# Twelve sublayers of a decoder on one core: in seven stage functions ScalarE, and no longer VectorE, scales the normalised rows

## The chip, the cores and the metric

The kernel runs on one core of a Trainium2 chip, in one launch. The metric is the device time of that launch in microseconds (us), lower is better; it is given as the median of several runs. A core has TensorE (matmuls and transposes, "PE" in the profile; "PEld" is its weight load), VectorE ("DVE"), ScalarE ("ACT"), GpSimd ("POOL") and SyncE ("SP", which here only issues transfers). Each engine takes its own instructions in the order in which they were put into its queue, and waits for another engine only through semaphores.

## What is computed

The reference takes `x` (4 rows of a batch, 512 positions, 128 channels, float32) through four layers of three sublayers. Every sublayer has the form below, with a normalisation over the 128 channels that has neither gain nor offset:

```python
def _layernorm(x, axis=-1, eps=1e-05):
    m = jnp.mean(x, axis=axis, keepdims=True)
    v = jnp.var(x, axis=axis, keepdims=True)
    return (x - m) / jnp.sqrt(v + eps)
...
x = x + sublayer(_layernorm(x))
```

The twelve sublayers, in order, with the name that their function has in the kernel: attention of a few selected queries (`l0_attn`), cross-attention with 77 context positions (`cross_attn`), local attention and a small feed-forward net, each twice (`f0_attn`, `f0_mlp`); attention (`l1_attn`), cross-attention (`cross_attn`), eight experts with a second normalisation inside (`l1_ffn`); attention over compressed, selected and windowed keys (`l2_attn`), masked cross-attention (`cross_attn`), a mixture of experts (`l2_ffn`); a selective scan (`l3_attn`), differential cross-attention (`l3_xattn`) and a last feed-forward net (`l3_ffn`). The sublayers mix positions of one row of the batch, never two rows. The data is in float32.

## The kernel before

**Two lanes.** The four rows of the batch are worked on by two lanes: lane 0 takes rows 0 and 2, lane 1 rows 1 and 3. Each lane has buffers and four banks of PSUM of its own. A lane goes through a layer's stages for one of its rows, then for the other one. `x` of all rows stays in SBUF, positions on the partitions: four tiles of 128 positions by 128 channels in each row of the batch. Most stages first need the normalised row transposed, channels on the partitions, which is `xnT` (128x512).

**The normalisation** has this chain, in `norm_stats`, `norm_pool`, `norm_apply`, `norm_tensor` and `norm_scalar`:

1. VectorE: `BN_STATS` of the four tiles (L467), then `BN_AGGR` of the four (L471), which gives mean and variance in `mv`.
2. GpSimd: variance plus epsilon in `vare` (L478), then to the power -1/2 in `rstd` (L479), both on 128x4 numbers.
3. VectorE: four times `tensor_scalar`, (x - mean) * rstd, 128x128 each, into `xn` (L487).
4. TensorE: four transposes into a bank of PSUM (L495), each as soon as its tile of `xn` is there.
5. ScalarE: one copy 128x512 from PSUM to `xnT` (L502).

**Who sets the order.** A stage function returns one generator for each engine. Each `yield` ends a piece; a piece begins with its waits. Before any instruction is issued, the generators of both lanes are run once against stand-ins of the engines (class `Meter`, and `Pool` for GpSimd), which only note waits, estimated costs (VectorE 0.18 us + 0.00104 us for each element of the width in a `tensor_scalar`, ScalarE 0.18 us + 0.00084 us in an activation, GpSimd 0.25 us + 0.002 us) and signals. `plan()` then runs a small greedy simulation: at each step it takes, among the next pieces of both lanes on all engines, the one that can begin first by these estimates. The order that results is the order in which the pieces are put into the queues of the engines. On the chip it is fixed: a piece whose wait isn't over holds up everything behind it on its engine, of the other lane too.

```python
                found.append((max(p[0], free[k[0]]), p[0] + p[1], k, p))
        begin, _, k, (_, took, signals, to) = min(found, key=lambda c: c[:2])
```

**Other lines that are spoken of.** L639 to L651 are VectorE's part of `l0_attn`: the value rows, then a search for the largest query norms (copy L642, MAX, MAX_INDEX and MATCH_REPLACE from L645, index map L651). L691 is its closing addition to `x`, L807 the row maximum of the first cross-attention. L724, L757 to L764 are the products and ScalarE's copies of cross-attention. L1149 is an activation of the small feed-forward net of layer 0. L1345 is GpSimd's memset of a value buffer in `l1_attn`. L1607, L1968, L2295 and L2483 are the closing additions of `l1_ffn`, `l2_attn`, `l3_attn` and `l3_xattn`. In `l3_attn` GpSimd multiplies (L2210), VectorE scans (L2277), and L2194 is the exponential on ScalarE.

## Time and profile before

| | |
|---|---|
| time, median of 3 runs | 2674.53 us (2669.82 to 2679.3) |
| the profiled execution: its time | 2670.86 us |
| the profiled execution: its span | 2669.0 us |
| TensorE busy | 1970.7 us, 74% |
| VectorE busy | 1740.5 us, 65% |
| ScalarE busy | 1016.6 us, 38% |
| GpSimd busy | 693.3 us, 26% |
| mean granted clock of TensorE | 0.815 of full speed |

The profile shows one execution. Its span goes from the first to the last recorded instruction; its time is 1.9 us longer. Busy shares are means over twelve stages with different limits. They don't say which engine ends a wait in a given stage, so the trace has to be read by stretches of time. A mean granted clock of 0.815 is a mean over stretches at full speed and at half of it.

### The profile page before, as it was taken

The page shows a single profiled execution, that of the slowest core. Times are in us where ns is not written, and L with a number is a line of the kernel's source. Part 1 is how long each engine was busy: PE and PEld are TensorE (multiplying, and loading weights), DVE is VectorE, ACT ScalarE, POOL GpSimd, SP SyncE. Part 2 cuts the span into 40 slices and gives each one's busy share as a digit, 9 for nine tenths or more (in the row PEclk, how much of TensorE's full clock was granted, in tenths as well). Part 3 has the DMA queues.
Part 4 walks back from the last instruction along what each step waited for, and adds up shares of the span by engine and source line. Part 5 has one row for each costly group of instructions (what it writes and reads, how often), then busy time and mean ns, then how long its engine had stood idle before and what let it go on. Part 6 is the DMA issues. An engine that isn't in the chain of part 4 may idle for free. (4 is left out here: it accounts for less than half of the span.)

```text
span 2669.0 us, 31475 instructions
## 1 busy us (share of the span) xinstructions
PE 1970.7 (74%) x11471; PEld 1135.5 (43%) x11474; DVE 1740.5 (65%) x3786; ACT 1016.6 (38%) x1606; POOL 693.3 (26%) x548
## 2 busy tenths in 40 slices
PE   4787888878777777799997577668866656677753
PEld 2453645445452232367665455545412222234331
DVE  6645657564655454433637787964579889986876
ACT  0235454555544343333333232232353544333422
POOL 0002323231320010000002443520136436445520
PEclk8787888989996686789998778766677877888875
DMA  3002111120220000000000000000000000000000
GB/s 148 1 1 52 40 48 44 32 60 23 69 83 1 1 1 1 12 10 1 1 1 1 1 1 1 1 1 1 0 0 0 0 0 0 1 1 1 1 5 12
DMA packets 19225, 43.86 MB, mean 16 GB/s; under 512 B 5323, under 2 KB 7935, under 8 KB 18175
## 3 DMA queue, kind: packets, MB, share of 16 engines
q1 hardware_dynamic: 19071, 41.86, 5.6%
q8 instruction: 91, 1.49, 0.2%
q14 instruction: 63, 0.52, 0.1%
HBM read 16.67 MB, written 1.05 MB: 7 GB/s over the span
## 5 line engine op out<-in xcount | busy, mean ns | idle before, releaser
L478 POOL TENSOR_SCALAR lane_vare<-lane_mv 128x4 f32<-128x4 f32 x64 | 18.0, 282 | 1098.0 <-DVE lane_mv L471 1097.9
L2134 PE MATMUL lane_banks<-l_attn_lane_hc,base 128*128 128x512 f32 x256 | 169.9, 781 | 114.2 <-DVE l_attn_lane_hc L2286 114.1
L2210 POOL TENSOR_TENSOR l_attn_lane_u<-l_attn_lane_xp,l_attn_lane_bn 128x512 f32<-128x512 f32 x128 | 181.2, 1441 | 228.6 <-ACT l_attn_lane_bn L2186 224.2
L2277 DVE TENSOR_TENSOR_SCAN l_attn_lane_h<-l_attn_lane_da,l_attn_lane_u 128x512 f32<-128x512 f32 x128 | 191.4, 1524 | 4.1 <-POOL l_attn_lane_u L2210 2.8
L1334 ACT ACTIVATE l_attn_lane_ex<-lane_banks 128x768 f32<-128x768 f32 (+3 forms) x128 | 86.8, 702 | 159.6 <-PE lane_banks L1292 158.9
L1526 ACT ACTIVATE l_ffn_lane_hT<-lane_banks,weights 128x512 f32<-128x512 f32 x128 | 87.9, 687 | 151.1 <-PE lane_banks L1482 150.6
L2134 PEld LDWEIGHTS lane_banks<-l_attn_lane_hc,base 128*128 128x128 f32 x256 | 56.8, 241 | 191.7 <-DVE l_attn_lane_hc L2286 156.8
L1573 DVE SCALAR_TENSOR_TENSOR l_ffn_lane_eo<-lane_banks,l_ffn_lane_sel,l_ffn_lane_eo 128x128 f32<-128x128 f32 x224 | 63.0, 344 | 110.0 <-PE lane_banks L1504 110.0
L1504 PEld LDWEIGHTS lane_banks<-weights,l_ffn_lane_hT 128*128 128x128 f32 x1024 | 120.5, 192 | 26.8 <-issue 24.8
L1504 PE MATMUL lane_banks<-weights,l_ffn_lane_hT 128*128 128x128 f32 x1024 | 123.4, 277 | 8.3 <-DVE l_ffn_lane_eo L1573 6.6
L2342 PE MATMUL lane_banks<-l_xattn_lane_km,l_xattn_lane_qT 128*128 128x462 f32 (+1 forms) x192 | 96.1, 604 | 41.2 <-DVE l_xattn_lane_sc L2455 33.8
L2186 ACT ACTIVATE l_attn_lane_bn<-lane_banks 128x512 f32<-128x512 f32 x64 | 38.1, 596 | 209.0 <-PE lane_banks L2128 205.8
L1831 POOL TENSOR_TENSOR l_attn_lane_qb<-l_attn_lane_qT,base 128x512 f32<-128x512 f32 x64 | 84.5, 1333 | 103.9 <-PE lane_banks L1733 66.5
L873 PE MATMUL lane_banks<-f_attn_lane_work,weights 128*128 128x512 f32 x128 | 76.9, 721 | 32.7 <-ACT f_attn_lane_work L988 32.7
L1394 DVE TENSOR_REDUCE l_attn_lane_mx<-lane_banks 128x4 f32<-128x2048 f32 (+2 forms) x64 | 93.2, 1487 | 9.2 <-PE lane_banks L1273 8.9
L1027 POOL TENSOR_TENSOR f_attn_lane_work<-f_attn_lane_work,f_attn_lane_rden 128x512 f32<-128x512 f32 x64 | 66.4, 1041 | 108.7 <-DVE f_attn_lane_rden L1071 108.7
L1742 PE MATMUL lane_banks<-base,l_attn_lane_sc 128*112 128x128 f32 x256 | 53.1, 345 | 53.2 <-POOL l_attn_lane_sc L1844 48.9
L1379 DVE RECIPROCAL l_attn_lane_rden<-lane_banks 128x16 f32<-128x16 f32 x16 | 4.1, 253 | 133.1 <-PE lane_banks L1244 133.1
L2194 ACT ACTIVATE l_attn_lane_da<-l_attn_lane_dt,a 128x512 f32<-128x512 f32 x128 | 86.4, 714 | 4.8 <-DVE l_attn_lane_h L2277 4.7
L1733 PE MATMUL lane_banks<-l_attn_lane_kall,l_attn_lane_qb 128*128 128x112 f32 x512 | 78.9, 307 | 11.2 <-DVE l_attn_lane_sc L1957 8.6
L487 DVE TENSOR_SCALAR lane_xn<-x,lane_mv,lane_rstd 128x128 f32<-128x128 f32 x176 | 61.6, 443 | 37.0 <-POOL lane_rstd L479 36.9
L2286 DVE TENSOR_TENSOR l_attn_lane_hc<-l_attn_lane_h,lane_banks 128x512 f32<-128x512 f32 x128 | 81.4, 671 | 4.3 <-PE lane_banks L2136 4.1
(518 smaller groups left out, 4972.1 us busy)
## 6 DMA issues: line engine op xcount, KB each, us to landing
f_attn_lane_work<-f_attn_lane_work SPq DMA_DIRECT2D x256, 64.0 KB, 2.0
weights<-packed SPq DMA_DIRECT2D x1, 4564.5 KB, 19.9
f_attn_lane_vb<-f_attn_lane_va SPq DMA_DIRECT2D x8, 512.0 KB, 4.5
f_attn_lane_vb<-f_attn_lane_va SPq DMA_DIRECT2D x8, 384.0 KB, 5.8
weights<-packed SPq DMA_DIRECT2D x1, 2320.0 KB, 8.0
weights<-packed SPq DMA_DIRECT2D x1, 2091.0 KB, 13.2
out<-x SPq DMA_DIRECT2D x4, 256.0 KB, 2.4
weights<-packed SPq DMA_DIRECT2D x1, 897.0 KB, 9.5
```

Of the source, the lines that this page charges most:

```text
L1334: act.activation(ex[:, kt % 2, h:h + 2, 0:T - P * kt], banks(0, 2)[:, :, 0:T - P * kt], ACT.Exp, scale=scale)\
L1394: v.tensor_reduce(mx[:, j, t, :], banks(0, R)[:, :, 0:n], AX.X, ALU.max).then_inc(*s.up("row_max"))
L1504: last = pe.matmul(ps(2)[:, tile(t)], hT[:, n % 2, c, tile(t)], w("m1_w2", (2 * (e - 1) + c) * D, (2 * (e - 1) + c + 1) * D), start=(c == ...
L1526: act.activation(hT[:, n % 2, c, :], ps(c), ACT.Relu, bias=w("m1_b1", b, b + 1)).then_inc(*s.up("hidden_ready"))
L1733: last = pe.matmul(ps(j % 2)[:, g * C:(g + 1) * C], qb[:, j % 2, tile(g)], kall[:, j, :], start=True, stop=True)
L1831: g_.tensor_tensor(qb[:, j % 2, :].rearrange("p (h q) -> p h q", h=A2_H), bc(qT[:, 32 * j:32 * j + 32], A2_H), w("headmask").rearrange("p ...
L2134: pe.matmul(ps(2 + c), w("ident"), hc[:, c, :], start=(n == 1), stop=(n == NS)).then_inc(*s.up("state_added"))
L2194: act.activation(da[:, i % 3, :], dt[:, c, :], ACT.Exp, scale=net.a3[:, c, n:n + 1]).then_inc(*s.up("da_ready"))
L2210: g.tensor_tensor(u[:, i % 3, :], dtx[:, c, :], bn[:, n % 2, :], ALU.mult).then_inc(*s.up("u_ready"))
L2277: v.tensor_tensor_scan(h[:, c, :], da[:, i % 3, :], u[:, i % 3, :], 0.0, ALU.mult, ALU.add).then_inc(*s.up("scanned"))
L2286: v.tensor_tensor(hc[:, c, :], h[:, c, :], ps(1), ALU.mult).then_inc(*s.up("hc_ready"))
L2342: pe.matmul(score_bank(u), qT[:, tile(t)], km[:, half * H + lo:half * H + hi, :].rearrange("p m k -> p (m k)"), start=True, stop=True).the ...
```

## The change

In seven stage functions (`l0_attn`, `cross_attn`, `l1_attn`, `l1_ffn`, `l2_attn`, `l2_ffn`, `l3_xattn`; `cross_attn` serves three stages) step 3 of the chain leaves VectorE. GpSimd works out `less` = -mean (128x4) before L478, and after L479 multiplies it by `rstd` in a piece of its own, which waits for `rstd_ready`. ScalarE then computes the four tiles of `xn` as Identity(rstd * x + less), with scale and bias taken from columns of one number a partition. That is 9 stages times 4 rows, 36 normalisations and 144 tiles. `l3_attn`, `f0_attn`, `f0_mlp`, `l3_ffn` and the inner normalisation of `l1_ffn` keep the form before. All numbers of lines below L500 grow by 7 to 16.

```diff
-def norm_pool(ln, s, g, tag=""):
+def norm_pool(ln, s, g, tag="", center=False):
+
     yield
     g.wait_ge(*s.at(tag + "variance_ready", 1))
+    if center:
+        ln.pool_steps.step(g.tensor_scalar(ln.less[:, :], ln.mv[:, :, 0], -1.0, None, ALU.mult))
     ln.pool_steps.link(g.tensor_scalar(ln.vare[:, :], ln.mv[:, :, 1], LN_EPS, 0.0, ALU.add, ALU.add))
     g.tensor_tensor(ln.rstd[:, :], ln.vare[:, :], ln.net.w("neghalf", 0, NT), ALU.pow).then_inc(*s.up(tag + "rstd_ready"))
+    if center:
+        yield
+        g.wait_ge(*s.at(tag + "rstd_ready", 1))
+        g.tensor_tensor(ln.less[:, :], ln.less[:, :], ln.rstd[:, :], ALU.mult).then_inc(*s.up(tag + "less_ready"))
...
+def norm_scale(ln, s, act, src):
+    yield
+    act.wait_ge(*s.at("less_ready", 1))
+    for t in range(NT):
+        act.activation(ln.xn[:, t, :], src[:, t, :], ACT.Identity, scale=ln.rstd[:, t:t + 1], bias=ln.less[:, t:t + 1])\
+           .then_inc(*s.up("norm_ready"))
...
     def scalar(act):
         enter(act)
+        yield from norm_scale(ln, s, act, x)
         yield from norm_scalar(ln, s, act, ps(0))
...
     def gpsimd(g):
         enter(g)
-        yield from norm_pool(ln, s, g)
+        yield from norm_pool(ln, s, g, center=True)
         g.memset(va[:, :, :, A1_HD + 1:32], 0.0).then_inc(*s.up("va_zeroed"))
         g.memset(va[:, :, :, A1_HD:A1_HD + 1], 1.0).then_inc(*s.up("va_zeroed"))
...
         yield from norm_stats(ln, s, v, x)
-        yield from norm_apply(ln, s, v, x, ln.xn)
```

The last three hunks are those of `l1_attn`; the other six functions differ in the same three places. In `l1_attn` the memsets now stand behind GpSimd's second wait. In the cross-attentions `norm_scale` stands behind the copies of the keys.

The planner is given the new pieces with their estimates, so its simulation comes out otherwise from the first stage on, and all engines' orders change with it. Three places follow, all on VectorE. Names are those of the buffers (`lane_` and `l_attn_lane_` are of either lane).

The first is the first pair of rows in `l0_attn`, at the program's start. Before:

```order
L467 BN_STATS lane_bn<-x 128x6 x4
L471 BN_AGGR lane_mv<-lane_bn 128x2 x4
L639 TENSOR_TENSOR l_attn_lane_v<-lane_banks,weights 128x512
L487 TENSOR_SCALAR lane_xn<-x,lane_mv,lane_rstd 128x128 x4
L642 COPY l_attn_lane_qn<-lane_banks 16x512
L645 MAX l_attn_lane_top<-l_attn_lane_qn 16x8
```

Changed (L661 to L667 are L645 to L651 before, L472 is L471, L673 builds the selection matrix):

```order
L661 MAX l_attn_lane_top<-l_attn_lane_qn 16x8
L662 MAX_INDEX l_attn_lane_topi<-l_attn_lane_top,l_attn_lane_qn 16x8
L665 CAST l_attn_lane_topf<-l_attn_lane_topi 16x32
L666 MEMSET l_attn_lane_topf 16x1
L667 TENSOR_TENSOR l_attn_lane_idxd<-weights,l_attn_lane_topf 16x512
L472 BN_AGGR lane_mv<-lane_bn 128x2 x4
L673 TENSOR_SCALAR l_attn_lane_onehot<-lane_banks,base 128x512 x4
```

The second lane's `BN_AGGR`, which stood ahead of the first lane's search, now stands behind all of it.

The second is the first rows' end of `l2_attn`. Before, the first lane's closing addition L1968 and, 49 rows further on, the second lane's:

```order
L1965 TENSOR_TENSOR x<-x,weights 128x512
L1968 TENSOR_TENSOR x<-x,lane_banks 128x512
L467 BN_STATS lane_bn<-x 128x6 x4
L471 BN_AGGR lane_mv<-lane_bn 128x2 x4
L1957 TENSOR_TENSOR l_attn_lane_sc<-lane_banks,l_attn_lane_mask 128x448
L487 TENSOR_SCALAR lane_xn<-x,lane_mv,lane_rstd 128x128 x4
```

```order
L1943 TENSOR_TENSOR l_attn_lane_tokens<-lane_banks,weights 128x512
L1947 TENSOR_REDUCE l_attn_lane_oT<-l_attn_lane_tokens 128x128
L1965 TENSOR_TENSOR x<-x,weights 128x512
L1957 TENSOR_TENSOR l_attn_lane_sc<-lane_banks,l_attn_lane_mask 128x448 x2
L1968 TENSOR_TENSOR x<-x,lane_banks 128x512
```

Changed (L1984 is L1968 before, L1959 and L1963 are L1943 and L1947, L468 is L467); directly ahead of these rows stands the first lane's L1984:

```order
L468 BN_STATS lane_bn<-x 128x6 x4
L472 BN_AGGR lane_mv<-lane_bn 128x2 x4
L1959 TENSOR_TENSOR l_attn_lane_tokens<-lane_banks,weights 128x512
L1963 TENSOR_REDUCE l_attn_lane_oT<-l_attn_lane_tokens 128x128
L1959 TENSOR_TENSOR l_attn_lane_tokens<-lane_banks,weights 128x512
L1963 TENSOR_REDUCE l_attn_lane_oT<-l_attn_lane_tokens 128x128
L1981 TENSOR_TENSOR x<-x,weights 128x512
L1870 TENSOR_TENSOR l_attn_lane_turns<-lane_banks,weights 128x512
L1871 TENSOR_TENSOR l_attn_lane_turns<-lane_banks,weights 128x512
L1872 TENSOR_TENSOR l_attn_lane_kp<-l_attn_lane_turns 128x512
L1881 COPY l_attn_lane_gl_172<-lane_banks 32x48
L1984 TENSOR_TENSOR x<-x,lane_banks 128x512
```

The second lane's closing addition now stands 12 rows behind the first lane's, where it stood 53 rows behind. Counted in the same way over the program, the closing additions of `l3_attn` (L2295) stand at rows 1701, 1770, 1851 and 1917 before and 1649, 1676, 1769 and 1799 after; those of `l3_xattn` (L2483) at 2008, 2046, 2142 and 2201 before and 1913, 1924, 2028 and 2042 after.

## Rows read from the trace of the kernel before

**Rows 1.** Busy time in four stretches (from:to, length, engines, clock, DMA share, GB/s):

```profile
1156.00:1282.00 126.00, 123.36 (x685) 87.64 (x684) 51.47 (x206) 47.11 (x72) 2.54 (x4) 0.96 0.02 6
1438.00:1576.00 138.00, 85.81 (x667) 66.91 (x665) 112.28 (x229) 35.62 (x50) 60.67 (x38) 0.75 0.00 1
2587.00:2628.00 41.00, 17.05 (x83) 7.71 (x84) 37.83 (x132) 10.57 (x18) 2.53 (x4) 0.56 0.02 7
2628.00:2669.00 41.00, 9.89 (x51) 4.55 (x52) 21.15 (x72) 6.12 (x10) 1.27 (x2) 0.50 0.07 20
```

**Rows 2.** The page's groups, VectorE's scaling (busy us, mean ns | idle before):

```profile
L487 DVE TENSOR_SCALAR lane_xn<-x,lane_mv,lane_rstd 128x128 f32<-128x128 f32 x176 | 61.6, 443 | 37.0 <-POOL lane_rstd L479 36.9
```

**Rows 3.** Timelines, one chain in the first cross-attention (start, length, instruction, [wait before]):

```profile
169.67 0.24 POOL L478 TENSOR_SCALAR lane_vare<-lane_mv 128x4 f32<-128x4 f32 x1 [69.60 <-DVE lane_mv L471]
169.99 1.03 POOL L479 TENSOR_TENSOR lane_rstd<-lane_vare,base 128x4 f32<-128x4 f32 x1
171.12 1.12 DVE L487 TENSOR_SCALAR lane_xn<-x,lane_mv,lane_rstd 128x128 f32<-128x128 f32 x4 [0.25 <-POOL lane_rstd L479]
172.66 0.60 ACT L502 ACTIVATE lane_xnT<-lane_banks 128x512 f32<-128x512 f32 x1 [0.93 <-PE lane_banks L495]
```

**Rows 4.** Groups by line and shape, ScalarE, activations with one or two operands more:

```profile
L1149 ACT ACTIVATE f_mlp_lane_hT<-lane_banks,weights 128x512 f32<-128x512 f32 x8 | 6.2, 777 | 25.0 <-PE lane_banks L495 25.0
L760 ACT ACTIVATE cross_attn_lane_kT<-lane_banks 128x77 f32<-128x77 f32 x8 | 1.9, 235 | 11.9 <-PE lane_banks L718 11.9
L757 ACT ACTIVATE cross_attn_lane_kT<-lane_banks,weights 128x77 f32<-128x77 f32 x4 | 1.3, 326 | 21.2 <-PE lane_banks L718 21.2
L758 ACT ACTIVATE cross_attn_lane_kT<-cross_attn_lane_kT,weights 128x77 f32<-128x77 f32 x4 | 1.4, 360 | 0.1
```

**Rows 5.** Timelines, `l1_attn` and `l2_ffn`, long scalings and what GpSimd did:

```profile
945.37 1.33 POOL L1345 MEMSET l_attn_lane_va<- 128x1472 f32 x1
945.56 2.07 DVE L487 TENSOR_SCALAR lane_xn<-x,lane_mv,lane_rstd 128x128 f32<-128x128 f32 x4
1767.22 3.96 DVE L487 TENSOR_SCALAR lane_xn<-x,lane_mv,lane_rstd 128x128 f32<-128x128 f32 x4 [1.37 <-POOL lane_rstd L479]
```

**Rows 6.** Waits, VectorE from 1438 to 2587 us (idle us, waits, longest):

```profile
DVE lane_xn L487 <- POOL lane_rstd L479: 16.4, 14, 1.9
```

**Rows 7.** Timeline, VectorE, the first rows in `l0_attn` and the first cross-attention:

```profile
24.67 0.38 DVE L471 BATCH_NORM_AGGREGATE lane_mv<-lane_bn 128x2 f32<-128x6 f32 x4
40.02 0.68 DVE L651 TENSOR_TENSOR l_attn_lane_idxd<-weights,l_attn_lane_topf 16x512 f32<-16x512 f32 x1
170.19 0.69 DVE L691 TENSOR_TENSOR x<-x,lane_banks 128x512 f32<-128x512 f32 x1 [0.71 <-PE lane_banks L599]
176.28 0.48 DVE L807 TENSOR_REDUCE cross_attn_lane_mx<-lane_banks 128x4 f32<-128x308 f32 x1 [3.07 <-PE lane_banks L729]
```

**Rows 8.** Timeline, VectorE, closing additions of both lanes:

```profile
2070.81 0.68 DVE L2295 TENSOR_TENSOR x<-x,lane_banks 128x512 f32<-128x512 f32 x1
2144.82 0.69 DVE L2295 TENSOR_TENSOR x<-x,lane_banks 128x512 f32<-128x512 f32 x1 [0.87 <-PE lane_banks L2142]
2549.64 0.69 DVE L2483 TENSOR_TENSOR x<-x,lane_banks 128x512 f32<-128x512 f32 x1 [8.77 <-PE lane_banks L2379]
2586.38 0.69 DVE L2483 TENSOR_TENSOR x<-x,lane_banks 128x512 f32<-128x512 f32 x1 [4.97 <-PE lane_banks L2379]
```

**Rows 9.** Busy time of VectorE's scans L2277 alone, two stretches (busy us, count, clock):

```profile
2001.00:2063.00 62.00, 44.32 (x28) 0.78 0.00 0
2063.00:2128.00 65.00, 19.80 (x16) 0.82 0.00 1
```

**Rows 10.** Timeline, ScalarE in `l3_attn`, around one table load:

```profile
1970.78 0.71 ACT L2194 ACTIVATE l_attn_lane_da<-l_attn_lane_dt,a 128x512 f32<-128x512 f32 x1
1971.51 1.28 ACT L2164 ACT_TABLE_LOAD   x1
1972.80 0.63 ACT L2164 ACTIVATE l_attn_lane_sgc<-l_attn_lane_cv 128x512 f32<-128x512 f32 x1
```

More of the change, by code:

```diff
@@ L315, in __init__ @@
         self.rstd = net.sb(f"lane{index}_rstd", [P, NT])
+        self.less = net.sb(f"lane{index}_less", [P, NT])
         self.area = net.take(SCRATCH)
@@ L635, in vector @@
         yield from norm_stats(ln, s, v_, x)
-        yield from norm_apply(ln, s, v_, x, ln.xn)
         yield
@@ L760, in scalar @@
             act.activation(kT[:, :], ps(1, 0, S2), ACT.Copy).then_inc(*s.up("k_ready"))
+        yield from norm_scale(ln, s, act, x)
         yield from norm_scalar(ln, s, act, ps(0))
@@ L780, in gpsimd @@
         enter(g)
-        yield from norm_pool(ln, s, g)
+        yield from norm_pool(ln, s, g, center=True)
     def vector(v):
@@ L1306, in scalar @@
         enter(act)
+        yield from norm_scale(ln, s, act, x)
         yield from norm_scalar(ln, s, act, ps(0))
@@ L1343, in gpsimd @@
         enter(g)
-        yield from norm_pool(ln, s, g)
+        yield from norm_pool(ln, s, g, center=True)
         g.memset(va[:, :, :, A1_HD + 1:32], 0.0).then_inc(*s.up("va_zeroed"))
@@ L1358, in vector @@
         yield from norm_stats(ln, s, v, x)
-        yield from norm_apply(ln, s, v, x, ln.xn)
         for i, name in enumerate("qk"):
@@ L1510, in scalar @@
         enter(act)
+        yield from norm_scale(ln, s, act, x)
         yield from norm_scalar(ln, s, act, ps(0))
@@ L1537, in gpsimd @@
         enter(g)
-        yield from norm_pool(ln, s, g)
+        yield from norm_pool(ln, s, g, center=True)
         yield from norm_pool(ln, s, g, tag="out_")
@@ L1544, in vector @@
         yield from norm_stats(ln, s, v, x)
-        yield from norm_apply(ln, s, v, x, ln.xn)
         def logits():
@@ L1772, in scalar @@
         act.activation(mask[:, :, 0:C - A2_M], w("a2_seen").rearrange("p (j k) -> p j k", j=J), ACT.Copy).then_inc(*s.up("seen_ready"))
+        yield from norm_scale(ln, s, act, x)
         yield from norm_scalar(ln, s, act, ps(0))
@@ L1822, in gpsimd @@
         enter(g_)
-        yield from norm_pool(ln, s, g_)
+        yield from norm_pool(ln, s, g_, center=True)
         g_.memset(kp[:, 0:32], 0.0).then_inc(*s.up("pad_ready"))
@@ L1850, in vector @@
         yield from norm_stats(ln, s, v, x)
-        yield from norm_apply(ln, s, v, x, ln.xn)
         def rope(dst, signal):
@@ L2025, in scalar @@
         enter(act)
+        yield from norm_scale(ln, s, act, x)
         yield from norm_scalar(ln, s, act, ps(0))
@@ L2039, in gpsimd @@
         enter(g)
-        yield from norm_pool(ln, s, g)
+        yield from norm_pool(ln, s, g, center=True)
     def vector(v):
@@ L2045, in vector @@
         yield from norm_stats(ln, s, v, x)
-        yield from norm_apply(ln, s, v, x, ln.xn)
         yield
@@ L2386, in scalar @@
         act.activation(kT[:, :], ps(1, 0, S2), ACT.Identity, bias=w("x3_bk")).then_inc(*s.up("k_ready"))
+        yield from norm_scale(ln, s, act, x)
         yield from norm_scalar(ln, s, act, ps(0))
@@ L2413, in gpsimd @@
         g.memset(va[:, :, :], 0.0).then_inc(*s.up("va_zeroed"))
-        yield from norm_pool(ln, s, g)
+        yield from norm_pool(ln, s, g, center=True)
         for i in range(UNITS + 2):
@@ L2430, in vector @@
         yield from norm_stats(ln, s, v, x)
-        yield from norm_apply(ln, s, v, x, ln.xn)
         yield
```

## The prediction

> **What bounds the kernel now.** I read the busy shares first (the table above). No engine is near its span: TensorE 74%, VectorE 65%, ScalarE 38%, GpSimd 26%. So the limit changes with the stage, and I cut the span into stretches [rows 1]. The reader is to see three kinds. In the experts of layer 1 TensorE works 123.36 of 126 us; nothing taken from VectorE can help there. In `l2_attn` VectorE works 112.28 of 138 us (81%) and TensorE 85.81; there VectorE's queue is the nearest to a limit. In the last 82 us everything waits for everything: at first VectorE is busy 37.83 of 41 us with both lanes, then, with one lane alone, only 21.15 of 41.
>
> Next the chain of the normalisation itself. The page's groups give all scalings into `xn`: 176 tiles, 61.6 us of VectorE, and 37.0 us of idle time ahead of them, 36.9 of it for GpSimd's power [rows 2]. 36 of its 44 groups of four change, 144 tiles, so 50 us (61.6 x 144/176) leave VectorE, 1.9% of the span. One chain in time order [rows 3]: L478 takes 0.24 us, L479 1.03, four scalings 1.12, and `xnT` is done at 173.26, 3.6 us after L478 began. A wait for `rstd` ends on every engine that has nothing else queued; where the lanes go in step, this chain lies on the path.
>
> **The change, part by part.** Every duration is of the profiled execution, and the sum is made against its time of 2670.9 us. That is 3.7 us under the median of 2674.5, so a result is moved up by 3.7 at the end.
>
> *One chain's latency.* GpSimd's `less` = -mean has the form of L478, so +0.24 us [rows 3]. The product with `rstd` isn't in the trace in this form on 128x4; it lies between L478's 0.24 and L479's 1.03, and as it has no power I take 0.24 plus 0.08, the gap between L478's end and L479's start: +0.32. ScalarE's Identity with both operands on 128x128 isn't in the trace either. A copy costs 0.60 us at 512 wide [rows 3] and 235 ns at 77 wide, so about 277 ns at 128. Scale and bias add 777 - 600 = 177 ns at 512 wide, the bias alone 326 - 235 = 91 ns, and with SBUF as source it is 360 where a bias costs 326, 34 more [rows 4]. 277 + 177 + 34 = 0.49 us a tile. Four lie between 1.7 us (overlapping like VectorE's) and 2.0 us (end to end), against 1.12: +0.6 to +0.9. I take +0.6, since the transposes follow tile by tile. A chain thus grows by 1.2 us, bounds 0.8 and 2.2 (the product at 1.03, the tiles end to end).
>
> (a) *Stages in which the lanes go in step* (`l0_attn`, first and second cross-attention, `l1_attn`, `l1_ffn`): ten pairs of chains, of which a pair exposes one. In the two pairs of `l1_ffn` TensorE at 98% hides it [rows 1]. Eight times 1.2 is +9 us. Against it: in `l1_attn` a scaling took 2.07 us beside GpSimd's memset of 1.33 us [rows 5], 0.95 more than the usual 1.12. The memset now comes after the product and ScalarE does the scaling. Four such, two exposed: -2. Together +7.
>
> (b) *Stages in which they don't* (`l2_attn`, third cross-attention, `l2_ffn`, `l3_xattn`): 16 chains. VectorE gets back 16 x 1.12 = 18 us. In this part of the span it waited 16.4 us for the power before the scalings [rows 6]; 16 of the 20 chains there change, so 13 us go. Of the 61.6 us, 44 x 1.12 = 49.3 are the usual time; 12.3 are longer ones, 3.8 of that in `l1_attn`, and of the rest I give these stages a good half, 5 us (the longest took 3.96 [rows 5]). In all 36 us. VectorE is busy 81% there, so the most that can reach the end is 29, and nothing is possible too, as the lane whose chain it is doesn't get its rows sooner. I take half, 18. The chains' own growth, 16 x 1.2 = 19 us, lies under the other lane's work but for VectorE's idle fifth: +4. Together -14.
>
> (c) *The early order.* The second lane's `BN_AGGR` ran at 24.67 and will now run behind the first lane's search, which ended at 40.70 [rows 7]: up to 16 us later. Most of it was waiting for the same search anyway. What is newly uncovered is the lane's way from variance to its own search: 3.6 us up to `xnT` [rows 3] and some 2.4 for product, copy and sum, so +6. In the cross-attentions the second lane's closing addition, at 170.19, will stand behind the first lane's row maximum, which ended at 176.76 [rows 7]: 5.9 us later at most, but the addition's lane has GpSimd, transposes and products of its own to go through beside the other's; I take +1 for each of two pairs. Together +8, bounds 2 and 25. GpSimd, ScalarE and TensorE have the second lane's chain queued behind this wait, nothing of the first lane's before its selection.
>
> (d) *The late order.* From `l2_attn` on the lanes stand closer: 12 rows instead of 53. At the end they were 36.7 us and 59 rows apart [rows 8], now 14 rows. Alone, the last lane leaves VectorE idle 48% of the time [rows 1]. The part spent alone shrinks by 36.7 x 45/59 = 28 us, and at that idle share 28 x 0.48 = 13 us are saved; with its share for lost `l3_xattn` waits I take -16 (bounds 0 and -28). The price is in `l3_attn`, where the lanes were 74 us apart [rows 8], one lane's products beside the other's scans. With both scanning a scan takes 44.32/28 = 1.58 us, with one 19.80/16 = 1.24 [rows 9]. If the new order puts 40 to 65 more of the scans beside the other lane's, that is +14 to +22; I take a bit over half of the lower, +8, because the order says who stands beside whom but not for how long. Together -8.
>
> The changed kernel's order has eight table loads fewer on ScalarE, all in `l3_attn`. A load takes 1.28 us, and the activation before it ended at 1971.49, the one after began at 1972.80: 1.31 us from the one to the other [rows 10]. That is 10 us of an engine which is busy under half of the time there, and I count nothing. The Trainium skill (ScalarE: Activation LUTs, What ACT_TABLE_LOAD costs) puts a drain of 1380 ns on top, 2.66 us a switch; eight would be 21 us and, if a fifth of it showed, 4 us less in the sum. These rows leave no room for such a drain.
>
> Sum: +7 - 14 + 8 - 8 = -7: 2664 for a profiled run, **2667 us** as a median.
>
> **The rivals.**
>
> *A. The relief counts in full.* For it: VectorE at 81% in `l2_attn`, and 37 us of idle time that no longer exist. Against it: the other engines wait in the same chain. Then (b) is -29 + 4, (d) is -16, table loads half their 10: +7 - 25 + 8 - 16 - 5 = -31, 2640, as a median 2643; between 2630 and 2652.
>
> *B. Slower: scans in step.* One mechanism, in `l3_attn`: both lanes arrive together, scan together and do their products together. 65 scans more at 0.34 us are +22, and the stretch in which one prepares while the other scans, which kept VectorE at work (19.80 us of scans in 65), falls away: +10 for the two rounds. The tail's gain halves, -8. With (a) +7, (b) -14 and (c) +8: +25, 2696, as a median 2699; between 2688 and 2705. It decides from about 45 more scans in step on. For it: the closing additions of `l3_attn` are 27 and 30 rows apart instead of 69 and 66. Against it: the planner's own costs see VectorE's queue. The Trainium skill speaks for this rival (GPSIMD Engine Reference, 1. Specifications): GpSimd shares its SBUF interfaces with VectorE and contends with its instructions that have two SBUF inputs, as a scan has. The scans' 1.58 beside 1.24 us agree.
>
> *C. ScalarE's queue.* The scaling now waits for GpSimd at the head of ScalarE's queue, and the other lane's exponentials and copies stand behind it; before, ScalarE waited only for the transposes. 36 times 1.2 us, half of it felt, is +22 in place of part (b)'s +4: +11 on the whole, 2682, as a median 2685; between 2678 and 2692. Against it: ScalarE has 35.62 us in 138 of `l2_attn` [rows 1].
>
> *D. Nothing to see.* A reordering of 2669 us of work for 50 us of one engine ends within 8 us of before: 2667 to 2682.
>
> **How the numbers follow.** Forecast (2655 to 2680) 0.38, A 0.20, B 0.22, C 0.10, D 0.10. 0.3% is 8 us, about what a measurement of this kernel tells from no change: 2666.5 and 2682.5. Faster: A's 0.20, half of the forecast (0.19), a little of D: 0.41. Slower: B 0.22, C 0.08, the bounds of (c): 0.32. The same: 0.27. The range leaves out A's lower third and B's upper quarter, with some 0.05 for what I haven't seen: 2640 to 2698.
>
> **What would show it.** Right: four scalings on ScalarE in 1.7 to 2.0 us, a product of about 0.3 us; the second lane's first `BN_AGGR` after 40 us; the end of `l0_attn` some 6 us later; from `l2_attn` to the end a stretch shorter by about 20 us; a tail alone of about 15 us. Wrong: scans at a mean near 1.58 through all of `l3_attn` (B); VectorE waiting longer for ScalarE's copies in `l2_attn` than before (C); the kernel level with before up to `l3_attn` (a and c too dear); the lanes drifting apart on the chip although the order has them close (d).

## The result, and the profile after

The changed kernel takes 2714.5 us (median of 4 runs, 2714.0 to 2719.9) where the kernel before takes 2674.7. The ratio is 1.0154, 95% interval 1.0132 to 1.0176: slower by 1.5%, some 40 us. The forecast was 2667 with a range up to 2698.

The page's busy times, and then the page's groups of the changed normalisation:

```profile
PE 2007.0 (74%) x11471; PEld 1158.7 (43%) x11474; DVE 1690.0 (62%) x3642; ACT 1061.4 (39%) x1742; POOL 718.9 (26%) x620
```

```profile
L503 ACT ACTIVATE lane_xn<-x,lane_less,lane_rstd 128x128 f32<-128x128 f32 x144 | 59.2, 482 | 107.5 <-POOL lane_less L487 107.5
L487 POOL TENSOR_TENSOR lane_less<-lane_less,lane_rstd 128x4 f32<-128x4 f32 x36 | 9.9, 274 | 3.0 <-POOL lane_rstd L483 0.2
```

VectorE fell by 50.5 us, from 1740.5 to 1690.0, as forecast. A tile costs ScalarE 482 ns, where the forecast had 490. What the forecast had no term for is the first number: TensorE is busy 36.3 us longer, with the same 11471 matmuls. Some of that is the choice of run: the changed kernel's profiled run, at 2719.9 us and a granted clock of 0.798, is the longest of its four, and that of the kernel before, at 0.815, is below its median.

The chain in the first cross-attention, timelines of GpSimd, ScalarE, VectorE and TensorE (to be read beside [rows 3, 7]):

```profile
177.76 0.69 DVE L707 TENSOR_TENSOR x<-x,lane_banks 128x512 f32<-128x512 f32 x1 [3.46 <-PE lane_banks L615]
179.68 0.26 DVE L810 COPY cross_attn_lane_vt<-lane_banks 77x128 f32<-77x128 f32 x1
179.95 0.24 POOL L481 TENSOR_SCALAR lane_less<-lane_mv 128x4 f32<-128x4 f32 x1 [71.02 <-DVE lane_mv L472]
180.27 0.24 POOL L482 TENSOR_SCALAR lane_vare<-lane_mv 128x4 f32<-128x4 f32 x1
180.59 1.04 POOL L483 TENSOR_TENSOR lane_rstd<-lane_vare,base 128x4 f32<-128x4 f32 x1
181.71 0.20 POOL L487 TENSOR_TENSOR lane_less<-lane_less,lane_rstd 128x4 f32<-128x4 f32 x1
181.94 1.65 ACT L503 ACTIVATE lane_xn<-x,lane_less,lane_rstd 128x128 f32<-128x128 f32 x4 [2.59 <-POOL lane_less L487]
184.80 2.07 PE L740 MATMUL lane_banks<-lane_xnT,weights 128*128 128x512 f32 x2 [0.69 <-ACT lane_xnT L518]
189.59 0.48 DVE L823 TENSOR_REDUCE cross_attn_lane_mx<-lane_banks 128x4 f32<-128x308 f32 x1 [9.65 <-PE lane_banks L745]
190.18 0.68 DVE L707 TENSOR_TENSOR x<-x,lane_banks 128x512 f32<-128x512 f32 x1
```

GpSimd's part now takes 1.96 us (179.95 to 181.91) instead of 1.35, the four tiles 1.65 instead of 1.12. VectorE copies the values right after the statistics, then stands idle 9.65 us for the scores, and only then closes the second lane's `l0_attn`: 12.4 us after the first lane's, where 2.7 us lay between them before. VectorE's waits for the scores, in all cross-attentions that wait in this way (idle us, waits, longest), before and changed:

```profile
DVE cross_attn_lane_mx L807 <- PE lane_banks L729: 41.7, 8, 6.7
```

```profile
DVE cross_attn_lane_mx L823 <- PE lane_banks L745: 76.2, 8, 9.9
```

That growth has two sources. In the experiments below the changed work in before's order (oldorder_newwork) waits 60.9 us, and before's work in nearly all of the changed order (neworder_oldwork) waits 47.0. In this order:

```profile
DVE cross_attn_lane_mx L852 <- PE lane_banks L773: 60.9, 8, 9.2
```

```profile
DVE cross_attn_lane_mx L852 <- PE lane_banks L773: 47.0, 8, 6.9
```

**Where the time went, by stage.** I took the mean of both lanes' closing additions as a stage's end, for two profiled runs 49 us apart (2669.0 and 2718.1). `l0_attn` of the first rows: +9.5. From there to the end of the first feed-forward: +3.7, and +3.0 for its second rows. `l1_attn` +4.2, second cross-attention +10.7, `l1_ffn` +11.0, `l2_attn` -1.4, third cross-attention and `l2_ffn` -8.4, `l3_attn` +19, `l3_xattn` -4.8, the rest +2.6. There is no single place. At the end of the second cross-attention both lanes are 31 us late. From `l1_ffn` on the changed order brings the lanes closer together, and then the split depends on the measure: by the later lane alone `l3_attn` is +12 and the rest +14. Only the sum of these stages, +18, can be used there.

### The profile page after: what moved, and what is told of

Same layout as the page of the kernel before. It is cut to its first block and busy times, and to the rows that moved or that the text cites. A ratio compares the mean times of both kernels' runs of the same rounds, so it can differ in the third digit from the quotient of the medians.

```text
span 2718.1 us, 31517 instructions
## 1 busy us (share of the span) xinstructions
PE 2007.0 (74%) x11471; PEld 1158.7 (43%) x11474; DVE 1690.0 (62%) x3642; ACT 1061.4 (39%) x1742; POOL 718.9 (26%) x620
## 5 line engine op out<-in xcount | busy, mean ns | idle before, releaser
L2226 POOL TENSOR_TENSOR l_attn_lane_u<-l_attn_lane_xp,l_attn_lane_bn 128x512 f32<-128x512 f32 x128 | 189.3, 1509 | 150.5 <-ACT l_attn_lane_bn L2202 140.7
L481 POOL TENSOR_SCALAR lane_less<-lane_mv 128x4 f32<-128x4 f32 x36 | 11.4, 316 | 705.2 <-DVE lane_mv L472 704.9
L2293 DVE TENSOR_TENSOR_SCAN l_attn_lane_h<-l_attn_lane_da,l_attn_lane_u 128x512 f32<-128x512 f32 x128 | 194.0, 1559 | 4.0 <-ACT l_attn_lane_da L2210 1.9
L2358 PE MATMUL lane_banks<-l_xattn_lane_km,l_xattn_lane_qT 128*128 128x462 f32 (+1 forms) x192 | 93.4, 595 | 14.3 <-DVE l_xattn_lane_sc L2471 12.7
L503 ACT ACTIVATE lane_xn<-x,lane_less,lane_rstd 128x128 f32<-128x128 f32 x144 | 59.2, 482 | 107.5 <-POOL lane_less L487 107.5
L1758 PE MATMUL lane_banks<-base,l_attn_lane_sc 128*112 128x128 f32 x256 | 56.6, 364 | 55.7 <-POOL l_attn_lane_sc L1861 50.5
```

Source lines behind the costliest of these rows:

```text
L2226: g.tensor_tensor(u[:, i % 3, :], dtx[:, c, :], bn[:, n % 2, :], ALU.mult).then_inc(*s.up("u_ready"))
L2293: v.tensor_tensor_scan(h[:, c, :], da[:, i % 3, :], u[:, i % 3, :], 0.0, ALU.mult, ALU.add).then_inc(*s.up("scanned"))
L2358: pe.matmul(score_bank(u), qT[:, tile(t)], km[:, half * H + lo:half * H + hi, :].rearrange("p m k -> p (m k)"), start=True, stop=True).the ...
```

## The experiments

Ratios are those of a kernel's runs to runs of the kernel before on the same chip; 0.1% is 2.7 us. The experiments ran on four chips, on which the median of the kernel before was 2674 to 2679 us, so two experiments are compared by their ratios and not by their medians. "Work" means the instructions of the normalisation (before's or the changed), "order" the sequence in the queues. For the first runs the planner is run with one kernel's pieces and the instructions issued are the other's:

```diff
 def norm_scale(ln, s, act, src):
     yield
+    if not moved(s, act):
+        if isinstance(act, Meter):
+            act.wait_ge(*s.at("rstd_ready", 1))
+        return
     act.wait_ge(*s.at("less_ready", 1))
```

`moved` looks a stage up in a list `PLAN` in the planner's pass and in a list `RUN` when instructions are issued; the parts of GpSimd and VectorE are split in the same way.

**Before's order, changed work** (oldorder_newwork: PLAN empty, RUN all seven functions).

> All instructions of the changed kernel (ScalarE scales, GpSimd makes less), but the planner is run with the pieces of the kernel before, so that every engine's queue has before's order; ScalarE's scaling and GpSimd's product are set in where rstd is ready. Theory 1, the loss is the new order: the time is that of before within 15 us, 2660 to 2690, and the cross-attentions end as before. Theory 2, the loss is the longer chain on GpSimd and ScalarE (with a slower granted clock after each longer wait of TensorE): 2700 to 2720, as the changed kernel. In between, near 2695, the two share it.

2701.9 us, ratio 1.0077 (1.0057 to 1.0096). The median lies at the lower end of theory 2's range, but the ratio is half of the loss, 21 us of 41: so neither theory alone. Half of the loss is there without any change of order.

**Changed order, before's work** (neworder_oldwork: the reverse).

> All instructions of before (VectorE scales), but the planner is run with the pieces of the changed kernel, and VectorE's scaling is a place of its own behind rstd. All queues then have the changed order but for 262 of VectorE's 3574 instructions, nearly all in the cross-attentions, where the second lane's closing addition stays ahead of the first lane's row maximum. Theory 1 (order): 2690 to 2715, less than the changed kernel by what the cross-attentions cost it, about 15 to 20 us. Theory 2 (longer chain): 2665 to 2685, as before.

2695.2 us, 1.0055 (1.0034 to 1.0075). The order costs too, 15 us, inside the range of theory 1. So both are true at once, and with 21 and 15 us they make up most of the 41. One piece of the changed order is not in this run, as the expectation says: the two lanes close the second rows' `l0_attn` 2.7 us apart here, as before, and not 12.4.

**One piece of cross_attn cut in two** (split_after, on the changed kernel).

```diff
         else:
+            yield
             v.wait_ge(*s.at("scores_in_psum", 1))
             st.link(v.tensor_reduce(mx[:, :], scores, AX.X, ALU.max))
```

> The changed kernel with one more yield in VectorE's part of cross_attn, between the copy of the values and the row maximum, which were one piece. The planner can then put the other lane's closing addition and statistics between them. Theory 1a, the planner gives VectorE to one lane from the copy to the row maximum, 9.65 us idle each time, because the scaling that stood in front of this piece is gone: the three cross-attentions (12 rows) get back 3 to 5 us in each of the first two stages' pairs, 12 to 20 us in all, 2695 to 2702. Theory 2 (longer chain): within 4 us of the changed kernel.

2687.1 us, 1.0032 (1.0020 to 1.0044): 27 us by the medians and 33 by the ratios for one `yield`, more than expected. VectorE's timeline in the place shown above:

```profile
174.43 0.69 DVE L707 TENSOR_TENSOR x<-x,lane_banks 128x512 f32<-128x512 f32 x1 [3.46 <-PE lane_banks L615]
176.35 0.25 DVE L810 COPY cross_attn_lane_vt<-lane_banks 77x128 f32<-77x128 f32 x1
177.15 0.69 DVE L707 TENSOR_TENSOR x<-x,lane_banks 128x512 f32<-128x512 f32 x1 [0.54 <-PE lane_banks L615]
185.65 0.48 DVE L824 TENSOR_REDUCE cross_attn_lane_mx<-lane_banks 128x4 f32<-128x308 f32 x1 [6.32 <-PE lane_banks L745]
```

The second lane's closing addition is 2.7 us behind the first's again, and the two chains overlap. The waits for scores fall to 32.4 us, under the 41.7 of the kernel before. By stage ends the first two cross-attentions (the first counted from the end of the first rows' `l0_attn`) were together 16 us longer in the changed kernel than before, and here they are 14 us shorter than before. So about half of what the cut gives back is something that the kernel before was paying too.

**The kernel before with a hop of 0.14 us in the planner** (hop14_before: `HOP = 0.15` becomes 0.14).

> The kernel before, all its instructions, with the planner's estimate of a hop between engines 0.14 us instead of 0.15, nothing else. Its order then falls from l2_attn on into nearly the same sequence as the changed kernel's (closing additions at the same rows from the end of l2_ffn to the end). Theory 1b, the late order alone (lanes close together from l2_attn on) costs, whatever brings it about: 2685 to 2700. If the late order is worth nothing either way: within 5 us of before. If the lanes' closeness gains, as my forecast had it: 2655 to 2668.

2666.3 us, 0.9947 (0.9930 to 0.9964): 12 us less by the medians, 14 by the ratio, with before's work. At the end of `l2_attn` this run is 1.6 us behind before, so the gain comes later. The last closing additions of `l3_xattn` are 13.0 us apart instead of 36.7, and the mean time of a scan rises from 1524 to 1572 ns, 4 us in all. What my expectation called theory 1b fell. Only the last part of the changed order is tested in this way: up to the end of `l2_attn` the closing additions from `l1_ffn` on stand at before's places in VectorE's queue. neworder_oldwork, which has the lanes close together from `l1_ffn` on, was some 14 us late at the end of the second cross-attention and some 27 us late at the end of the program, in one profiled run.

**GpSimd's part alone** (oldorder_pool: before's order, GpSimd makes `less`, VectorE still scales but waits for it).

```diff
-    v.wait_ge(*s.at("rstd_ready", 1))
+    v.wait_ge(*s.at("less_ready" if moved(s, v) else "rstd_ready", 1))
```

> Order of before in every queue and VectorE scales as before, but GpSimd works out less and its product as in the changed kernel, and VectorE's scaling waits for that product: GpSimd's part of the longer chain alone, 0.56 us a chain in the small ones. In the order of before the whole change of work cost 0.77% (about 20 us). Theory P, each added piece of latency costs by its length: 0.56 of some 1.2 us, so 8 to 12 us, 2684 to 2690. Theory Q, it is ScalarE's share that costs (tiles longer than VectorE's, other work of ScalarE behind the wait): within 4 us of before. Theory R, forecast's: late stages hide it, early ones show 8 x 0.56: +4 us, all of it before l2_attn.

2698.2 us, 1.0092 (1.0064 to 1.0121): as much as all of the changed work. The upper end of theory P is passed; Q and R fall. VectorE's busy time, 1740.1 us, is that of before (1740.5), so the small instructions on GpSimd didn't slow VectorE's own.

**Twice GpSimd's part** (pool_twice: two multiplications by one behind it, which leave `less` as it is).

> Order of before, VectorE scales as before and waits for less, and GpSimd makes less in four small instructions instead of two (two multiplications by one more, each waiting for the one before): another 0.6 us a chain. If time grows with the chain's length, about 24 us for 0.56 and as much again: 2718 to 2728. If the first 0.56 us tipped something over and more costs only its hidden remainder: 2700 to 2708.

2715.8 us, 1.0157 (1.0121 to 1.0193). GpSimd's timelines, first this run, then the one before it:

```profile
170.09 0.22 POOL L489 TENSOR_SCALAR lane_less<-lane_mv 128x4 f32<-128x4 f32 x1 [67.37 <-DVE lane_mv L472]
172.43 0.22 POOL L503 TENSOR_SCALAR lane_less<-lane_less 128x4 f32<-128x4 f32 x1
```

```profile
170.72 0.24 POOL L489 TENSOR_SCALAR lane_less<-lane_mv 128x4 f32<-128x4 f32 x1 [68.68 <-DVE lane_mv L472]
172.47 0.20 POOL L501 TENSOR_TENSOR lane_less<-lane_less,lane_rstd 128x4 f32<-128x4 f32 x1
```

1.95 us in oldorder_pool, 2.56 in pool_twice, 1.35 before [rows 3]; the medians are 1.96 and 2.57 over the 36 changed chains, and 1.35 over all chains of the kernel before. So 0.60 us more a chain cost 0.92%, 25 us or 0.68 us for each of 36 chains; 1.21 us more cost 1.57%, 42 us or 1.17 for each. The time of the second run lies between the two ranges of its expectation. As a total the cost is proportional within the intervals, and about the full added length. By stage it is not. The order is the same in these runs, so stage ends can be compared; these are us over before, one profiled run each, with act_only (described next) beside them:

| stage (changed chains) | oldorder_pool, +0.60 | pool_twice, +1.21 | act_only |
|---|---|---|---|
| `l0_attn` (4) | +1.0 | +0.4 | +0.9 |
| first cross-attention (4) | +2.7 | +4.4 | +0.2 |
| `f0_attn`, `f0_mlp` (0) | -3.0 | +2.3 | -1.5 |
| `l1_attn` (4) | +2.7 | +2.4 | +0.5 |
| second cross-attention (4) | +4.5 | +7.1 | +4.3 |
| `l1_ffn` (4) | +0.7 | +2.8 | +0.2 |
| `l2_attn` (4) | +3.4 | +11.1 | -3.8 |
| third cross-attention, `l2_ffn` (8) | +2.7 | +0.4 | -3.3 |
| `l3_attn` (0) | +0.3 | +0.4 | +0.9 |
| `l3_xattn` (4) | +10.5 | +12.7 | +10.0 |
| `l3_ffn` and the end (0) | +2.1 | +0.1 | +2.6 |

Four chains at full length would be 2.4 and 4.8 us. `l3_xattn` loses over four times that in the first run and little more in the second, `l0_attn` hides most of it, and the third cross-attention with `l2_ffn` hid it in pool_twice. The stages without a changed chain show how much a single run scatters, some 3 us.

**ScalarE's part alone** (act_only; it leaves out `less`, the bias column is the mean itself, so its numbers aren't those of the reference).

> Order of before, ScalarE scales, GpSimd does no more than before. Left out: less; the activation adds the mean itself as its bias instead of -mean times rstd, so the numbers differ, the instructions' sizes don't. ScalarE's scaling waits for rstd, not for less, so a chain grows by ScalarE's 0.5 us alone, and VectorE's 50 us are gone. If GpSimd's part is what costs: 2670 to 2682, level with before. If ScalarE's longer tiles and its queue cost too and VectorE's relief is worth nothing: 2685 to 2695. If the relief is worth what the forecast said (18 us and more): 2650 to 2665.

2680.4 us, 1.0006 (0.9987 to 1.0025): level. Either the longer tiles on ScalarE and the 50 us less on VectorE cancel out, or neither is worth anything; the total can't tell. By stage (table above) something is won in `l2_attn` and behind it, and 10 us are lost in `l3_xattn`.

**The changed work in the late stages alone** (late_only: RUN is `l2_attn`, `l2_ffn`, `l3_xattn`).

> Order of before, the whole changed work, but only in l2_attn, l2_ffn and l3_xattn (12 of the 36 chains); the rest has before's work. The forecast's step (b) had -14 us for these stages with the third cross-attention. The stage times of the run with all of the changed work in this order say +10 for them: 2682 to 2690. The forecast's step: 2660 to 2668.

2689.0 us, 1.0055 (1.0033 to 1.0076): 12 of the 36 chains cost 15 us where step (b) had a gain. By stage ends 7.5 us are in `l3_xattn`, of 18 between the profiled runs. In all six runs with before's order and a longer chain in this stage it is 7 to 13 us longer, whether a chain grew by 0.5 or by 1.2 us; with before's work it isn't longer (fill_old below). In act_only the stretches (busy times, then the granted clock) show on what, before and then act_only:

```profile
2310.70:2568.00 257.30, 182.07 (x1066) 96.14 (x1067) 198.87 (x344) 89.49 (x126) 131.59 (x65) 0.85 0.00 1
```

```profile
2309.10:2576.50 267.40, 196.40 (x1066) 103.53 (x1067) 198.46 (x333) 94.22 (x138) 133.75 (x65) 0.79 0.00 1
```

The same 1066 matmuls take TensorE 14 us longer, at a granted clock of 0.79 instead of 0.85. In oldorder_pool TensorE is busy 7.5 us longer in this stage at 0.83, in pool_twice 10.9 at 0.81: most of what is lost here is TensorE's own time.

**A filler for TensorE** (fill_new: before's order, changed work; fill_old: before's work; fill_split2: further below).

```diff
+        if t == 0 and s.stage in STAGES and not isinstance(pe, Meter):
+            pe.wait_ge(*s.at("variance_ready", 1))
+            for _ in range(FILL):
+                pe.transpose(bank[:, tile(0)], ln.net.w("ident"), ln.net.w("ident"))
         pe.wait_ge(*s.at(tag + "norm_ready", t + 1))
```

`FILL` is 6.

> The changed kernel's work in the order of before, and ahead of each changed normalisation's transposes TensorE does six transposes of the identity (216 in all) as soon as the variance is there, into the bank that the transposes then overwrite: work of no use, put where TensorE waits for rstd and the scaling. So far TensorE's busy time grew by about as much as the span, for the same matmuls: 29 us of 30 with this work in this order. Theory K, a longer wait of TensorE lowers the granted clock, and the matmuls behind it take longer: the filler gives 10 to 20 us back against the run without it (2702), 2682 to 2692, at a higher mean clock in the cross-attentions. Theory L, the chain's length alone costs and the busy time grows with it for another reason: no gain, 2700 to 2715, since 216 transposes come on top.

> The same filler in the kernel before (its work, its order). Theory K: the waits are there before too, though shorter, so it gains as well, less than with the changed work: 2655 to 2670. Theory L: 2675 to 2690.

fill_new 2688.0 us, 1.0053 (1.0034 to 1.0071) against 1.0077 without: 6 us by the ratios, 14 by the medians, and the intervals overlap, so a gain is likely but not clear of the noise. fill_old 2675.1 us, 1.0007 (0.9985 to 1.0030): no gain, where theory K had at least 5 us. In fill_new the transposes of the identity took 40.3 us of a busy time of 1998.7; the kernel's own matmuls thus took 1958, 41 less than in oldorder_newwork (1999.4). A stretch of 46 us around the second cross-attention, without and with the filler (the matmuls in it aren't quite the same):

```profile
1113.90:1160.00 46.10, 35.19 (x120) 20.99 (x118) 13.66 (x63) 19.97 (x60) 7.23 (x16) 0.67 0.05 17
```

```profile
1113.90:1160.00 46.10, 34.42 (x144) 22.32 (x145) 14.96 (x65) 22.50 (x69) 8.94 (x20) 0.82 0.05 17
```

The clock is 0.82 instead of 0.67; from the end of `l1_attn` to the end of this stage it is 0.83 instead of 0.66, and there the filler gives 4.4 us back. In the kernel before the same stage has 0.75, in fill_old 0.85, and 1.5 us are won. In `l3_xattn` it gives 0.4 us. So the first half of theory K, a higher clock with work in the wait, holds in both; that it buys time is seen at most with the changed work and its longer waits.

**Both yields, both works** (split2_after, split2_before: the cut in cross_attn, and one `yield` ahead of each round of the search in `l0_attn`).

> The changed kernel with the yield in cross_attn of the run before, and one more yield ahead of each round of the search in l0_attn, so that the second lane's BN_AGGR needn't wait for all of the search. If the long search in one piece is what cost 6.5 us up to the end of the first rows of l0_attn: that many us less than with the first yield alone, 2680 to 2683. If it was the chain itself: within 3 us of 2687.

> The kernel before with the same two sets of yields. Its order then falls into nearly the same one as the changed kernel's with them, so the two runs differ by the work alone. From what the work costs in the order of before (0.77%), this one should be 15 to 25 us faster than the changed one with the same yields: 2655 to 2668. If the order decides alone, the two are level.

2683.8 us, 1.0034 (1.0016 to 1.0052), and 2651.0 us, 0.9924 (0.9902 to 0.9947). The search's cut gave nothing: the first rows' `l0_attn` ended at 100.5 us by the mean of the lanes, as without it, though `BN_AGGR` now stood ahead of the search's rounds. That expectation fell, and what keeps this stage 5 us longer with the changed work than with before's (95.4) wasn't taken apart. The two orders are nearly the same, 3158 of 3610 of VectorE's instructions beside the scaling stand at the same place, so the pair gives the price of the work in about a second order: 1.10%, against 0.77% in before's. The cuts help before's work too: this run is 20 us faster than before, and its first two cross-attentions are 19 us shorter by stage ends.

**The planner's costs corrected** (costs_after, costs_before, on the two kernels with both yields).

```diff
+        if op == ALU.pow:
+            return self.work(1.03 + 0.0 * width(out))
...
-        return self.work(0.18 + 0.00084 * width(out) + (0.2 if accum_out is not None else 0.0))
+        pointers = (not isinstance(bias, float)) + (not isinstance(scale, float))
+        return self.work(0.18 + 0.06 * pointers + 0.00084 * width(out) + (0.2 if accum_out is not None else 0.0))
```

> The changed kernel with both sets of yields and a planner whose costs are those measured here: 1.03 us for GpSimd's power instead of 0.26, 0.06 us more on ScalarE for a scale or bias in a column. The order of l3_attn to the end then is again close to that of before, the lanes far apart. If lanes close together gain, as hop14_before showed (-12 us), this one loses 5 to 15 us on the one with the plain costs: 2688 to 2697. If a plan with the right costs is better by itself, it is 5 to 15 us faster: 2668 to 2678.

> The kernel before with both sets of yields and the planner's corrected costs (power 1.03 us, 0.06 us for a column operand on ScalarE). The lanes stay close together at the end (closing additions of l3_xattn 15 and 17 instructions before the next lane's, 160 in the run with plain costs at one of them). The corrected costs gained 14 us for the changed work, most of it in the second rows of the local attention; if that holds here, 2635 to 2645; if it was luck of one order, 2648 to 2660.

> The kernel before with both sets of yields (2651 without filler) and the filler. Theory K: 2638 to 2650. Theory L: 2650 to 2662.

costs_after 2669.3 us, 0.9982 (0.9962 to 1.0001); costs_before 2641.1 us, 0.9874 (0.9848 to 0.9901); fill_split2 2663.3 us, 0.9953 (0.9932 to 0.9975), by the ratios 8 us slower than without filler, where theory K had a gain. By stage ends costs_after gains 14 us on split2_after, which has the same work, in the second rows of the first feed-forward and loses 17 and 8 in the two rounds of `l3_xattn`: each order has luck in one place and not in another. costs_before beats both kernels, by 34 us and by 73, with before's work. The two are 1.08% apart, but that isn't the price of the work alone: only 2376 of 3610 of VectorE's instructions stand at the same place in their two orders, and costs_after has the lanes far apart at the end.

## Why the prediction was wrong

**The sum.** The forecast had -7 us for the work, (a) and (b), and 0 for the order, (c) and (d). Measured in before's order the work is +21; the order with before's work is +15, without the one piece named above; some 5 are left for that piece and for the two together.

**The prices of the parts** were right: 50 us off VectorE; 1.65 us for four tiles where I had 1.7; 0.60 us on GpSimd where I had 0.56.

**"Lies under the other lane's work"**, in step (b), is where it failed most, and "ten pairs of chains, of which a pair exposes one", in (a), with it. I had 8 times 1.2 us exposed early (9.6, entered as 9) and 19 us of the late growth shrunk to 4. Measured, the 0.60 us of GpSimd alone cost 25 us, as much as if all 36 chains showed all of it, and 12 late chains with all of the changed work cost 15 us. VectorE busy 81% of the time in `l2_attn` was no cover: pool_twice lost 11.1 us there with four chains. That the total comes near 36 full lengths is in part luck, as stages show from almost nothing to four times the added length. The lanes share queues in a fixed order; my reading is that a chain that is late holds up the other lane's instructions behind it, so that both are late. The runs don't show that path. Part of the cost is TensorE: behind longer waits its granted clock is lower, and in `l3_xattn` its own busy time is most of what is lost. Overall the filler took back 6 to 14 us, with intervals that overlap.

**(b)'s relief**, 18 us: as a gain of the late stages it wasn't there, for late_only is +15 in three of the four stages where (b) had -14. act_only has the relief and ScalarE's +0.5 us a chain, and is level. If chains cost there what they cost in the GpSimd runs, 36 x 0.5 = 18 us, the relief was worth about as much over the whole kernel; that is an estimate, and no run has the relief alone. In `l2_attn` act_only is 3.8 us shorter than before, in the third cross-attention and `l2_ffn` 3.3.

**(c), the early order**: `l0_attn` +9.5 us for +6, and +8.2 with before's work in nearly the same order. The cross-attentions were priced +1 a pair, below a bound of 5.9 that came from before's wait of 3.07 us [rows 7]. In the changed kernel the wait itself was 9.65 us, and both cross-attentions together were 16 us longer, of which the work alone, in before's order, makes 10; that leaves some 6 where (c) had 2. The planner lets a lane keep an engine through a wait in the middle of a piece; the copy of the values and the row maximum are such a piece, and the scaling that stood ahead of it had delayed its start. Without the scaling it starts right after the statistics. The order's rows showed the place; I priced it with the wait of before. With the scaling back in its place, in neworder_oldwork, the two closing additions are 2.7 us apart again.

**(d), the late order**: -8 forecast, -12 to -14 measured in hop14_before, which has the late part of this order with before's work. The last closing additions are 13.0 us apart there, and the scans cost 4 us more where I had 8. That much of (d) was right. For the changed order as a whole it doesn't hold: with before's work it costs 15 us, not 0, and some 12 of the 27 us between the profiled runs come after the second cross-attention. No term had the lanes' new distance in `l1_ffn`, where by stage ends neworder_oldwork is 13 us longer.

**Rival A** fell with (b). **Rival B** had the direction but not the mechanism: 128 scans took 194.0 us instead of 191.4. `l3_attn` did grow, by 12 or 19 us according to the measure, but not through the scans. B's reading of [rows 9] also has another cause beside it: in the stretch with slow scans GpSimd was busy 44.45 of 62 us, in the other 24.53 of 65. Over the whole kernel before, the 57 scans with GpSimd busy during more than half of them took 1.82 us on average, the other 71 took 1.29. What it quoted from the Trainium skill (GPSIMD Engine Reference, 1. Specifications), that GpSimd contends with VectorE's instructions that have two SBUF inputs, agrees with this; but it is GpSimd and not the other lane's scan that stands beside the slow ones, and the change moved their total by under 3 us. **Rival C** fell: with the scaling waiting at the head of ScalarE's queue and nothing more on GpSimd, the time is level, and with GpSimd's part ScalarE's adds nothing to it (1.0077 beside 1.0092).

**Left open**: by which path a longer chain costs time, and why `l3_xattn` loses 7 to 13 us to any growth; which instructions of the new order keep `l0_attn` longer (with changed work in before's order it is 0.5 us shorter); and how the 11 us of `l1_ffn` divide (5 are there in before's order with the changed work, 13 in nearly the changed order with before's work, and the two don't add).

## What to carry to other kernels

A latency added to a short chain that every lane and every stage passes through isn't hidden because another engine is busy. Here, with the queues' order fixed, its full length times the number of passes came near the total, and that is the price to start from; but the stages shared it very unevenly, so no single stage can be priced so. Taking an instruction out can also take out the delay that kept a planner from handing an engine to a lane that must wait on it: in the new order, look at what now stands ahead of each wait, and how long that wait will be then, not how long it was. And where an order is planned from costs, measure the change of work in one fixed order before believing any difference: here a hop of 0.14 instead of 0.15 us was worth 12 to 14 us and one `yield` about 30.

## What was not expected of the hardware

TensorE's granted clock followed the gaps: in the second cross-attention 0.75 before, 0.66 with the longer waits and 0.83 with useless transposes in them, and the pair of 128x512 products behind the first chain took 2.07 us (184.80 in the timeline above) where before it took 1.13; TensorE's timeline of the kernel before:

```profile
173.31 1.13 PE L724 MATMUL lane_banks<-lane_xnT,weights 128*128 128x512 f32 x2 [0.69 <-ACT lane_xnT L502]
```

Full speed and half of it are 2.4 and 1.2 GHz. Busy time and span often moved together: +36 and +49 us for the changed kernel, +29 and +30 in before's order. The runs of one kernel show it too: 25 runs of the kernel before on one chip go from 2662 to 2685 us, and the longer ones have the lower clock, 0.818 down to 0.807. But it isn't a rule from one kernel to another. act_only's TensorE is busy 24 us longer in its profiled run, of which the span shows 11 and the median nothing; fill_old has a median clock of 0.815 against 0.811 of the kernel before on the same chip, and gained nothing; and costs_before, the fastest of all, has a median of 0.807.
